# Attention 0 of a two-block kernel: the reciprocal roots of the q and k variances as one power on GpSimd, and waits that a later event covers taken out

## The reference, cut to what matters

```
q  = _ln(q,  qln_w,  qln_b)      # 2 heads of 128 a group
qx = _ln(qx, qxln_w, qxln_b)     # 2 heads of 128 a group
k  = _ln(k,  kln_w,  kln_b)      # 1 head of 128 a group
kx = _ln(kx, kxln_w, kxln_b)     # 1 head of 128 a group
_ln(x, w, b) = (x - mu) * rsqrt(var + 1e-5) * w + b    # over a head's 128
core = softmax(q k / sqrt(128)) v;  xout = softmax(qx kx / sqrt(128)) vx
catq = fp8 roundtrip of clip(concat(core, xout) / smooth)
out  = catq @ wproj * (proj_in_scale * proj_w_scale)
x    = x + tanh(g) * out
```

## Time and profile before

| what | us |
|---|---|
| median of 3 runs (1654.69 to 1662.16) | 1658.83 |
| profiled execution | 1660.3 |
| span of its instructions | 1658.6 |
| PE busy in the span | 1416.0 (85%) |
| DVE busy | 1316.9 (79%) |
| ACT busy | 977.7 (59%) |
| POOL busy | 792.8 (48%) |

### The profile page before, as it was taken

How to read it: one execution, slowest core, us unless ns; L and a number is a source line. 1 busy time by engine, 2 the same in 40 slices (tenths; PEclk the granted TensorE clock), 3 DMA queues, 4 the chain that set the end, 5 groups by cost and what they waited for, 6 DMA issues and landing times. The chain is left out here.

```text
span 1658.6 us, 32346 instructions
## 1 busy us (share of the span) xinstructions
PE 1416.0 (85%) x11712; PEld 1205.5 (73%) x11712; DVE 1316.9 (79%) x2894; ACT 977.7 (59%) x1960; POOL 792.8 (48%) x1355
## 2 busy tenths in 40 slices
PE   0477899999999999999999997799959998996895
PEld 0466888888888888988888996567625554554895
DVE  7998998898898889988988999533337987786464
ACT  4676666666667666766666764422126565652673
POOL 2577555556555556565555554201103433331673
PEclk9878999999999999999999999799978998987898
DMA  3101000000000000000011000342154002002563
GB/s 96 39 13 33 14 14 20 14 14 21 27 2 20 27 17 17 15 21 14 14 21 49 2 2 1 119 58 29 38 103 95 1 14 64 1 14 85 182 236 121
DMA packets 60238, 69.98 MB, mean 42 GB/s; under 512 B 5424, under 2 KB 52784, under 8 KB 59952
## 3 DMA queue, kind: packets, MB, share of 16 engines
q1 hardware_dynamic: 57456, 60.54, 13.5%
q0 software_dynamic: 2432, 7.34, 1.3%
q10 hardware_dynamic: 192, 0.04, 0.0%
HBM read 55.56 MB, written 12.34 MB: 41 GB/s over the span
## 5 line engine op out<-in xcount | busy, mean ns | idle before, releaser
L901 POOL TENSOR_TENSOR RB<-YS,M 128x512 bf16<-128x512 f32 x128 | 148.4, 1159 | 220.3 <-DVE YS L769 220.2
L577 ACT ACTIVATE QT<-B,sm 128x256 f32<-128x256 f32 x256 | 130.2, 559 | 167.2 <-PE B L425 167.2
L444 PE MATMUL SS<-QT,KT 128*128 128x256 f32 x512 | 159.0, 406 | 20.0 <-DVE mx L717 19.7
L1768 POOL TENSOR_SCALAR_AFFINE_SELECT P<-P 128x1024 f32<-128x1024 f32 x64 | 82.0, 1281 | 159.6 <-ACT P L1618 159.6
L757 DVE SCALAR_TENSOR_TENSOR Y<-PO,RL,RSM 128x128 bf16<-128x128 f32 x512 | 144.2, 345 | 4.5
L460 PE MATMUL PO<-V,PPP 128*128 128x129 f32 x1024 | 142.9, 285 | 5.3 <-DVE Y L757 5.3
L393 PE MATMUL PA<-WH,XQ 128*128 128x256 f32 x512 | 140.8, 308 | 5.9 <-ACT SQ L603 5.9
L744 DVE TENSOR_TENSOR QN<-QN,yy 128x768 f32<-128x768 f32 x128 | 137.9, 1077 | 5.0 <-POOL yy L144 5.0
L460 PEld LDWEIGHTS PO<-V,PPP 128*128 128x128 f32 x1024 | 133.4, 203 | 6.0 <-issue 6.0
L131 POOL TENSOR_TENSOR ww<-yy 128x12 f32<-128x12 f32 x192 | 94.0, 489 | 86.8 <-DVE yy L152 76.8
L395 PE MATMUL PA<-WL,XQ 128*128 128x256 f32 x512 | 129.2, 286 | 0.0
(11 more groups left out here) (329 smaller groups left out, 4391.7 us busy)
## 6 DMA issues: line engine op xcount, KB each, us to landing
W<-in_w SPq DMA_DIRECT2D x16, 1024.0 KB, 8.1
Q<-qsc SPq DMA_DIRECT2D x48, 128.0 KB
WR<-in_wprojT SPq DMA_DIRECT2D x16, 256.0 KB, 3.0
K<-ksc SPq DMA_DIRECT2D x12, 256.0 KB
qsc<-T POOLq DMA_DIRECT2D x8, 384.0 KB, 4.2
X<-in_x SPq DMA_DIRECT2D x4, 512.0 KB, 5.7
CR<-in_xctxT SPq DMA_DIRECT2D x8, 256.0 KB, 2.9
RSM<-rsm_d SPq DMA_DIRECT2D x16, 128.0 KB, 3.9
```

The costliest lines, as they stand in the source:

```text
L444: pe.matmul(SS[:, 256 * z:256 * z + 256], k[:, 128 * z:128 * z + 128], q[:, 256 * z:256 * z + 256], start=True, stop=False)
L577: a.activation(QT[i % 2][:, o:o + 256], B1[:, o:o + 256], ACT.Identity, bias=col(n + "b"), scale=col(n + "w"))
L901: p.tensor_tensor(RB[i % 2][:], YS[:], M[:], ALU.subtract).then_inc(s_rb, 1)
```

## The change

The first guess and the Newton rounds go. POOL scales the 12 sums and adds eps itself, and raises them to the power -0.5 in one instruction against a tile that holds -0.5. The multiplication of the second item of a pair doesn't wait for the roots again. Thirteen further waits are taken out, each on an event that another wait of the same engine, or of the engine that it waits for, already implies. Two of them are in the stage of the second attention.

```diff
-        ww = sb("ww", [128, 12])
+        half = sb("half", [128, 12])
@@ pe_trans
-            if i:
-                pe.wait_ge(s_evk, i)
@@ pe_scores
-            pe.wait_ge(s_evk, i + 1)
             if i:
                 pe.wait_ge(s_ex, i)
+            else:
+                pe.wait_ge(s_evk, 1)
@@ pe_weigh
-            pe.wait_ge(s_ex, i + 1)
+            if i == N - 1:
+                pe.wait_ge(s_ex, N)
@@ act_evac
-            if i >= 2:
-                a.wait_ge(s_ST, i - 1)
@@ act_expo
-            if i >= 2:
-                a.wait_ge(s_LO, i - 1)
@@ act_turned
-            if i:
-                a.wait_ge(s_C, i)
@@ act_copy_square
-            if i >= 4:
-                a.wait_ge(s_T, i - 3)
-            if i >= 7:
-                a.wait_ge(s_LO, i - 6)
@@ dve_maximum, dve_add
-            if i >= 2:
-                v.wait_ge(s_ST, i - 1)
-            if i >= NB:
-                v.wait_ge(s_add, i - NB + 1)
@@ dve_reduce
-            if j >= 2 and h == 0:
-                v.wait_ge(s_rstd, j - 1)
             v.tensor_reduce(w_[:, 6 * h:6 * h + 6], SQ[:].rearrange("p (h d) -> p h d", d=128), AX, ALU.add).then_inc(s_red, 1)
-            if h:
-                v.wait_ge(s_red, i + 1)
-                v.tensor_scalar(w_[:], w_[:], 1.0 / 128, EPS, ALU.mult, ALU.add).then_inc(*vs.up())
-                v.wait_ge(*vs.at())
-                guess(v, w_[:], y[:], s_vguess)
@@ dve_mul
-            v.wait_ge(s_rstd, j + 1)
+            if h == 0:
+                v.wait_ge(s_rstd, j + 1)
@@ pool_rstd
-                p.wait_ge(s_vguess, j + 1)
-                newton(p, ps, vv[j % 2][:], yy[j % 2][:], ww[:], s_rstd)
+                v_ = vv[j % 2][:]
+                p.wait_ge(s_red, 2 * j + 2)
+                p.tensor_scalar(v_, v_, 1.0 / 128, EPS, ALU.mult, ALU.add).then_inc(*ps.up())
+                p.wait_ge(*ps.at())
+                p.tensor_tensor(yy[j % 2][:], v_, half[:], ALU.pow).then_inc(s_rstd, 1)
@@ pool_rounded
-            if i >= 2:
-                p.wait_ge(s_T2, i - 1)
@@ pool_attention_0
+            p.memset(half[:], -0.5).then_inc(*ps.up())
+            p.wait_ge(*ps.at())
@@ act_evac_out, dve_lower (second attention)
-            if u >= 2:
-                a.wait_ge(s_T2, N + u - 1)
-            if i >= 2:
-                v.wait_ge(s_LO, N + i - 1)
```

More of the change, by code:

```diff
@@ L260, in build @@
             sem(n) for n in ("w", "w1", "wsc", "wmean", "wcen", "wh", "wl", "w3a", "w3p", "w3", "ph", "pl"))
-        s_proja, s_proj, s_sqa, s_sqb, s_vev, s_red, s_vguess, s_rstd, s_mul, s_Tq, s_T, s_evk = (
-            sem(n) for n in ("proja", "proj", "sqa", "sqb", "vev", "red", "vguess", "rstd", "mul", "Tq", "T", "evk"))
+        s_proja, s_proj, s_sqa, s_sqb, s_vev, s_red, s_rstd, s_mul, s_Tq, s_T, s_evk = (
+            sem(n) for n in ("proja", "proj", "sqa", "sqb", "vev", "red", "rstd", "mul", "Tq", "T", "evk"))
         s_S, s_mx, s_ST, s_ex, s_LO, s_y0, s_ys, s_rb, s_T2, s_rt, s_C, s_add = (
@@ L728, in dve_reduce @@
             j, h = divmod(i, 2)
-            w_, y = vv[j % 2], yy[j % 2]
+            w_ = vv[j % 2]
             v.wait_ge(s_sqb, i + 1)
-            if j >= 2 and h == 0:
-                v.wait_ge(s_rstd, j - 1)
             v.tensor_reduce(w_[:, 6 * h:6 * h + 6], SQ[:].rearrange("p (h d) -> p h d", d=128), AX, ALU.add).then_inc(s_red, 1)
-            if h:
-                v.wait_ge(s_red, i + 1)
-                v.tensor_scalar(w_[:], w_[:], 1.0 / 128, EPS, ALU.mult, ALU.add).then_inc(*vs.up())
-                v.wait_ge(*vs.at())
-                guess(v, w_[:], y[:], s_vguess)
         def dve_mul(v, i):
```

## The result

| | us |
|---|---|
| before, median of 4 runs | 1657.84 |
| after, median of 4 runs (1594.88 to 1602.90) | 1600.11 |
| ratio after / before | 0.9657, 95% interval 0.9634 to 0.9680 |
| profiled execution after, its span | 1599.65, 1597.9 |

The forecast was 1599 us, the range 1580 to 1668. New are L876 (scaling and eps) and L878 (the power).

What follows compares the result with a forecast made beforehand. PE was taken to bound attention 0's loop, DVE close behind. Gains of 51 us (steady part), 9 (start) and 1 (after 900.8), 61 in all, took 1660.3 to 1599 us; range for 8 in 10: 1580 to 1668.

Steps and rivals of the forecast that it cites:

- The bound: Steady part of attention 0's loop: PE bounds it, busy 654.5 of 697.1 us, with DVE close behind at 627.8.
- the free steps: Loop steps in which PE runs matmuls without a gap: they stay at some 6.5 us, only the excess can go.
- the waits: The removed waits: costed at nothing, as PE has no gap at their places in a step without a stall.
- The thirds steps: Steps with L884, two a group: PE's 2.39 us stop falls to 1.0 us and the 1.64 us of clock go.
- The power: The single power on POOL over 12 columns: taken as 1.0 us, the middle of 0.21 and 1.81.
- second rival: Slower: a long power holds up DVE's L761 through the shared port; 1745 us at a 4.7 us power; chance 0.18.
- The port: DVE and POOL share one port pair under an exclusive lock, so a long power would stop L761 on DVE.
- The centring steps: Two a group, PE waiting 1.28 and 0.40 us for L717: both alike afterwards, 0.4 us of stall each.
- L444's waits for L717 down to 0.4 us: Sign for the forecast: PE's waits at L444 for DVE's maximum, 10.4 us in 12 in the steady part, shrink to this.
- The start: First 16 steps, 58.5 to 203.7 us, with the quantization beside: 9 us gained, bounds 3 and 20.
- the rest: After 900.8 us: 1 us gained; from 1000 us on, untouched but for two waits that cost nothing.
- The first: Rival, half of the gain: power takes 1.1 to 2.6 us, PE still stops 1.7 us or more; 1630 us, chance 0.24.

Runs made afterwards that it cites:

- experiment 1: Kernel before with only the thirteen waits and the second wait for the roots taken out, guess and Newton rounds kept; 1653.70 us, ratio 0.9979.
- experiment 7: Changed kernel with the centring's division of the means by 128 moved from DVE to POOL; 1576.72 us, ratio 0.9496 to the kernel before.
- experiment 5: Changed kernel with the power done twice in series on POOL, first into a tile nobody reads; 1690.01 us, ratio 1.0174 to the kernel before.
- experiment 3: Changed kernel with a constant start value and the Newton rounds on POOL in place of the power; 1659.35 us, ratio 1.0012 to the kernel before.

## Why the prediction was right, and where it was right by two errors

**The bound, the free steps, the waits: right.** The free step is 6.47 to 6.53 us in both kernels, only the excess went, and experiment 1 finds no gain in the loop from the waits; the 2 to 3 us that they cost with the power are below what the forecast could tell.

**The thirds steps: right, with a different account inside.** Forecast 1.0 us of excess each, measured 0.73. L749 ends at 576.22, 3.62 us behind its step's L468 (572.60), against 611.69 - 607.17 = 4.52 before: 0.9 us earlier, forecast 0.8. L857 does move its hold from L736 to L724. The first L864 takes 0.68 us instead of 1.39, as forecast. The clock no longer falls, and that was 20 us of the sum.

**The power: mis-sized.** I took 1.0 us, the middle of 0.21 and 1.81; it is 2.27 alone and 2.36 on average, over the bound that I had from L877. It takes 0.16 us a column, where the Newton instructions of this size took 0.2 us in all. It lies between the two marks that I had set (under 1.1 us right, over 2.5 us slower). By my own second rival 2.4 us should have eaten nearly all of DVE's slack.

**The port: the premise of the second rival fell.** It said that the power holds up L761 for as long as it runs. L741 starts 1.15 us after the power did, 1.1 us before its end, and takes 0.29 us; its mean over the steady part is 293 ns, and 36 of its 96 there run wholly inside a power. Elsewhere it can be held: it took 593 ns beside POOL's L835 at 148.77 us. "SBUF — State Buffer", section "Who interferes with whom", in the Trainium skill says that the lock is held for the whole instruction; L857 against L724 bears it out, the power does not. It isn't free of the other engine either: ten of the 48 powers of the steady part begin 0.10 to 0.11 us after L749, which reads two tiles, and take 2.74 us instead of 2.27 (rows in experiment 7), while an L749 that begins 2.13 us after a power neither waits nor holds it up. The likeliest reading is that a power has the port only while it fetches its columns, near its start, but no run tests that. This error and the one before it cancelled in the thirds steps, where the power ends 0.6 us before it is needed.

**The centring steps: too hopeful.** Forecast 0.4 us of excess each; measured 1.3 and 1.1 to 1.6, 15 us instead of 5, and the sign "L444's waits for L717 down to 0.4 us" did not come (0.9 to 1.3 us each). The step that failed is the one that had L744 lose its 0.95 us to L901 no longer, "after, both are alike". It still loses 0.75: behind four scalings and a power of 2.74 us, L882 starts at 550.30, 0.27 us before L724, and holds it until 551.46 as before (rows in experiment 7). And both are alike only because the second got worse: the multiplication ahead of it takes 1.65 us on average, 1.10 before. A power of 1.0 us, even with the 0.47 us that L749 costs it, would have ended at 549.1 and L882 would have been out of the way; this is worked out, not run. Experiment 7 shows another way out: with the hold still there, the two divisions off DVE free the steps. In the sum the centring steps cost 10 us more than forecast, the thirds steps 3 and the other slow stretches 4 less, so 25 us of excess stay instead of 22.

**The start and the rest.** 9.7 us against 9, a guess between wide bounds whose terms did not come out. Of the 4.18 us wait for L901 3.2 us are still there, and the three waits of L436 went from 10.1 to 8.8 us, not to 6. What came instead is mostly clock, 0.86 to 0.90: PE is busy 103.0 us instead of 108.4 with the same 855 matmuls, where I had 2 us. That the sum fits is luck. Then 1.2 against 1; and 1.9 us behind the loop that no step had, within what that stretch does by itself.

**The rivals' place.** The first had the power's length (1.1 to 2.6 us), but its stops of 1.7 us did not come: 0.3 us each. The second priced a long power as a hold on DVE. It hurts by POOL's own queue instead: L882 is late for PE's turn and for the relay, L724 for the roots, as experiment 5 shows at 1690 us, where the second rival's formula gives about 1745.

## What to carry to other kernels

A chain on an engine that is half idle can set the time of the whole when a hand-over between two other engines is queued behind it; look for what stands behind the chain in each queue, and price moving that as well as shortening the chain (here the power alone was worth 64 us, the moved relay with the two divisions 63, all together 94). Small instructions on a few numbers are dear where two engines lock each other out: on DVE, L736 took 0.18 us alone and 1.15 us behind L877. Before a power is used in place of products, measure it per column: at 12 columns it beats a chain of twelve dependent instructions, at 48 it would cost 8 us.

## What the runs showed of the hardware that was not expected

- A power on POOL takes 0.4 us and 0.16 us a column (581 ns for 1 column, 41.2 us for 256). It does not keep DVE's L741 out while it runs (293 ns inside it), though POOL's subtraction of the thirds does (0.6 us, experiment 5); but it is itself 0.47 us longer when it begins just after DVE's L749.
- The length of a stop does not alone decide whether the clock falls. In experiment 1 PE stopped 12 times for 2.31 us in the steady part, and 11 times the granted clock fell to 0.50 at the end of the stop; the mean was 0.97. In experiment 3 it stopped 12 times for 2.31 to 2.37 us, with 16 more stops of up to 1.0, and the clock fell 3 times; the mean was 0.99:

```profile
206.70:903.20 696.50, 641.14 (x6148) 598.13 (x6145) 624.94 (x1294) 473.86 (x1112) 421.78 (x880) 0.99 0.06 19
```

- The part behind the loop took 645 to 660 us in different profiles of nearly the same instructions.
